# Near key tiles turned on VectorE instead of TensorE, with new orders in the first projections, the opening and the last pair

## What is computed

```python
x = x + xattn(layernorm(x), ctx, Wq, Wk, Wv, Wo)

def xattn(latents, context, Wq, Wk, Wv, Wo):            # 128 x 512, 2048 x 512
    hidden = concatenate([context, latents], axis=1)     # 2176 rows = 17 key tiles of 128
    q = (latents @ Wq).reshape(b, q_len, 4, 8, 128)      # 4 kv heads, 8 query heads each
    k = (hidden @ Wk).reshape(b, kv_len, 4, 128)
    v = (hidden @ Wv).reshape(b, kv_len, 4, 128)
    attn = softmax(einsum("bqhgd,bkhd->bhgqk", q, k) / sqrt(128))
    return einsum("bhgqk,bkhd->bqhgd", attn, v).reshape(b, q_len, 4096) @ Wo
```

## Time and profile before

| | |
|---|---|
| median of 3 runs | 638.62 us (638.28 to 638.98) |
| profiled execution, its time | 638.21 us |
| span, first to last instruction | 636.5 us |
| granted TensorE clock, mean | 0.999 of full |
| PE busy | 623.0 us (98%) |
| DVE busy | 434.4 us (68%) |
| ACT busy | 337.5 us (53%) |
| POOL busy | 212.9 us (33%) |

### The profile page before, as it was taken

How to read it: one execution, slowest core, us unless ns; L and a number is a source line. 1 busy time by engine, 2 the same in 40 slices (tenths; PEclk the granted TensorE clock), 3 DMA queues, 4 the chain that set the end, 5 groups by cost and what they waited for, 6 DMA issues and landing times.

```text
span 636.5 us, 11116 instructions
## 1 busy us (share of the span) xinstructions
PE 623.0 (98%) x3968; PEld 531.6 (84%) x3968; DVE 434.4 (68%) x885; ACT 337.5 (53%) x617; POOL 212.9 (33%) x161
## 2 busy tenths in 40 slices
PE   8999999999999999999999989999999999999998
PEld 6888887888999899889998879998879778797573
DVE  3533135686777777778876669789884775958873
ACT  3413114668776777777777636656454454447110
POOL 0000000349676867687765522225022020200000
PEclk9999999999999999999999999999999999999999
DMA  8501012467777767776756939475866757697500
GB/s 265 214 0 34 1 55 66 103 176 205 191 192 191 190 165 179 188 203 156 214 137 168 355 133 267 160 304 195 295 210 255 265 204 262 246 367 289 217 1 18
DMA packets 29534, 116.69 MB, mean 183 GB/s; under 512 B 7680, under 2 KB 8064, under 8 KB 21936
## 3 DMA queue, kind: packets, MB, share of 16 engines
q1 hardware_dynamic: 28912, 115.03, 57.7%
q10 hardware_dynamic: 576, 1.05, 0.6%
HBM read 86.30 MB, written 0.26 MB: 136 GB/s over the span
## 4 chain that ended last, share of the span: by engine, by line
PE 84%; DVE 6%; issue 2%; ACT 2%; DMA 2%; SPq 2%; POOL 1%; ACTq 0%; DVEq 0%
PE ps L1716 20%; PE ps L1434 13%; PE ps L1436 12%; PE ps L1435 12%; PE ps L1756 9%; PE ps L1508 4%; PE ps L1591 2%; PE ps L1745 2%; PE ps L1866 2%; DVE prob_far L1081 2%; DMA ring<-ctx_t_dram 2%; SPq L351 2%; PE ps L1829 2%; DVE prob_far L1109 2%; DVE res L1121 1%
## 5 line engine op out<-in xcount | busy, mean ns | idle before, releaser
L1716 PEld LDWEIGHTS ps<-norm_t,ring 128*128 128x128 f32 x1152 | 131.6, 192 | 4.9 <-issue 4.1
L1716 PE MATMUL ps<-norm_t,ring 128*128 128x128 f32 x1152 | 133.2, 276 | 0.0
L507 POOL TENSOR_TENSOR pt_lo<-far_t,pt_hi 128x512 fp32r<-128x512 f32 x86 | 102.2, 1203 | 61.6 <-ACT pt_hi L609 61.3
L1265 DVE SCALAR_TENSOR_TENSOR acc<-raw,cw,acc 128x127 f32<-128x127 f32 (+2 forms) x240 | 83.4, 424 | 18.8 <-ACT acc L879 18.2
L1081 DVE TENSOR_SCALAR_CACHE_REDUCE prob_far<-ps 128x1024 f32<-128x1024 f32 x64 | 73.8, 1155 | 31.9 <-PE ps L1436 31.6
L686 ACT ACTIVATE prob_far<-prob_far,neg_max 128x1024 f32<-128x1024 f32 x64 | 69.8, 1091 | 25.7 <-DVE neg_max L1085 25.6
L609 ACT ACTIVATE pt_hi<-far_t 128x512 fp32r<-128x512 f32 x90 | 51.3, 587 | 36.7 <-PE ps L1436 33.9
L1109 DVE STREAM_TRANSPOSE prob_far<-prob_far 128x1920 f32<-128x1920 f32 x30 | 65.0, 2171 | 0.1
L1434 PE MATMUL ps<-k_hi,q_hi 128*128 128x512 f32 (+2 forms) x160 | 62.4, 390 | 2.0 <-DVE prob_far L1081 1.6
L1434 PE MATMUL ps<-pt_hi,v_hi 128*128 128x256 f32 x208 | 61.1, 294 | 2.1 <-POOL pt_lo L507 1.2
L583 POOL TENSOR_SCALAR_AFFINE_SELECT at_hi<-a_hi 128x2048 fp32r<-128x2048 f32 x8 | 16.1, 2011 | 133.9 <-PE ps L1728 102.8
(11 more groups left out here) (213 smaller groups left out, 1213.8 us busy)
## 6 DMA issues: line engine op xcount, KB each, us to landing
ring<-w_in_dram SPq DMA_DIRECT2D x36, 1024.0 KB, 4.9
far_t<-prob_far SPq DMA_DIRECT2D x240, 120.0 KB, 2.3
ring<-w_out_dram SPq DMA_DIRECT2D x16, 1024.0 KB, 4.8
ring<-wq_dram SPq DMA_DIRECT2D x16, 512.0 KB, 4.2
ring<-wo_dram SPq DMA_DIRECT2D x16, 512.0 KB, 3.6
w_sb<-w_dram SPq DMA_DIRECT2D x4, 896.0 KB, 9.1
ring<-ctx_t_dram SPq DMA_DIRECT2D x3, 1024.0 KB, 6.9
ring<-w_dram SPq DMA_DIRECT2D x3, 1024.0 KB, 7.5
```

The source lines that it names most:

```text
L507: sub = lambda dst, a, hi: pool.tensor_tensor(dst, a, hi, ALU.subtract)
L1265: ins = nc.vector.scalar_tensor_tensor(a[:, i, back:], r[:, i, 0:T - back], cw[:, bass.ds(tile + i, 1), 3 - back:4 - back].rearrange("p a ...
L1716: ins = mm(ps[:, bank, t * T:t * T + T], w[:, t, c, :], norm_t[:, c, :], start=(c == 0), stop=(c == NC - 1))
```

## The change

All 17 key tiles, near ones too, are turned by VectorE and moved by DMA: `FAR_T` goes from 15 to 17, `turn_far` covers 2176 columns and waits for all three exponentials of its head, and `transposes`, both `near_split`s and the `near` tiles are gone. Units are renumbered: 0 and 1 are the plain tiles 13 to 16, which need only the move; 2 to 8 are split ones, on four slots in turn. GpSimd has seven remainders a pair, but VectorE takes unit 5 in the first step of a head (from n = 4 on) and unit 7 in the second. The orders on TensorE, ScalarE and VectorE change: the first exponential piece of the second head comes last on ScalarE, after the rounding of q; the first scores piece of pair n + 2 is evacuated in step n behind a block transpose; two chunks of scores lead in front of unit 0. `moves(m)` waits for TensorE's values of pair m - 2.

In the opening, the values of the last context block are made one tile at a time between the scores of pairs 0 and 1, and the latents' values come last. For the first context block VectorE rounds the context while ScalarE rounds Wk, TensorE does all high products first, and four more identity matmuls are made once the first quarter has landed. The first values are made in three passes over four banks. Cut to its core (removed helpers and buffers left out):

```diff
-FP32_TILES = {1: (13, 14), 2: (15, 16)}
+FP32_TILES = {0: (13, 14), 1: (15, 16)}
-FAR_T = (KV_LEN - NEAR) // P
+FAR_T = NKT
-SCORES_LEAD = {1: (2,)}
-SCORES_AT = {0: (1,), 2: (3, 4), 3: (5,), 4: (6, 7), 5: (8, 9)}
-LAST_SCORES_AT = {0: (1,), 2: (3, 4, 5), 3: (6, 7, 8, 9)}
+SCORES_LEAD = {0: (1, 2)}
+SCORES_AT = {1: (3, 4), 2: (5,), 3: (6, 7), 4: (8, 9)}
+LAST_SCORES_AT = {1: (3, 4, 5), 2: (6, 7, 8, 9)}
+LOW_U = {0: 5, 1: 7}
+SLOTS = 4
+WARM_SPLIT = 4
+def slot_of(p, u):
+    return (FAR_UNITS * p + u - FAR0) % SLOTS
+def by_dve(n, u):
+    return n > 0 and LOW_U.get(n % PAIRS) == u
 # SP, moves(m)
                 if m >= 2:
-                    sp.wait_ge(pfl_ok, FAR_UNITS * (m - 1))
+                    sp.wait_ge(pv_ps, UNITS * (m - 1))
+                elif m == 1:
+                    sp.wait_ge(kv_ps, 34)
 # GpSimd, a step
-                far_split(n, 3)
-                far_split(n, 4)
+                for u in (2, 3, 4):
+                    far_split(n, u)
+                if p == 0 and kv:
+                    v_split(kv, 2)
+                else:
+                    far_split(n, 5)
                 if n:
                     wo_split(n - 1, n - 1)
-                far_split(n, 5)
...
-                far_split(n, 7)
+                if p != 1:
+                    far_split(n, 7)
 # ScalarE, a step (the new order)
+                first_fars(n, kv, p)
                 if not begin:
                     output_split(n, b)
+                far(n, p, 4)
+                far(n, p, 5)
+                if not begin:
+                    wo_split(n - 1, 2 * kv + (p - 1) // 2, (p - 1) % 2)
...
                 soft_exp(n + 2, b, 0, 1)
+                if ask:
+                    far(n, p, 6)
...
+                soft_exp(n + 2, b, 0, 2)
+                soft_exp(n + 2, b, 0, 0)
+                far(n, p, 7 if ask else 6)
...
+                if ask:
+                    far(n, p, 8)
...
+                soft_exp(n + 2, b, 1, 1)
+                if not ask:
+                    far(n, p, 7)
...
                 soft_exp(n + 2, b, 1, 2)
+                if ask:
+                    q_split(n + 3, 1 - b, 6 + (1 - b))
+                soft_exp(n + 2, b, 1, 0)
...
+                if p == 3:
+                    act.wait_ge(pv_ps, 9 * n + 6)
+                    v_split(kv + 1, 1)
                 if not ask:
-                    soft_exp(n + 2, b, 1, 0)
+                    far(n, p, 8)
 # VectorE
-                dve.wait_ge(exp_ok, 2 * NPC * m + 3 * h + 2)
+                dve.wait_ge(exp_ok, 2 * NPC * m + 3 * h + 3)
...
                 turn_far(n + 1, 1 - b, 1)
+                scores_out(n + 2, b, 0, 0, sent)
...
                 scores_out(n + 2, b, 0, 2, sent)
-                scores_out(n + 2, b, 1, 0)
+                scores_out(n + 2, b, 1, 0, sent)
+                if p == 0 and not (isinstance(n, int) and n == 0):
+                    far_split(n, p, LOW_U[0])
                 scores_out(n + 2, b, 1, 1, sent)
                 scores_out(n + 2, b, 1, 2, sent)
-                if not ask:
-                    near_split(n + 1)
+                if p == 1:
+                    far_split(n, p, LOW_U[1])
                 if ask:
                     turn_far(n + 2, b, 0)
                     q_split(n + 3, 1 - b, 6 + (1 - b))
-                    near_split(n + 1)
-                    scores_out(n + 3, 1 - b, 0, 0)
 # TensorE, first block
+            pe.wait_ge(first_in[0], 32)
+            for _ in range(WARM_SPLIT):
+                mm(ps[:, 7, 0:P], ident[:], ident[:], start=True, stop=True)
             for c in range(NC):
+                pe.wait_ge(first_hi, c + 1)
+                pe.wait_ge(first_ctx, c + 1)
+                first_keys(c, wk_hi, ctx_hi[0], c == 0, False)
+                pe.wait_ge(first_lo, 2 * c + 1)
+                first_keys(c, wk_lo, ctx_hi[0], False, False)
                 pe.wait_ge(first_lo, 2 * c + 2)
-                for kv in range(KVH):
-                    ins = keys(0, kv, c)
+                first_keys(c, wk_hi, ctx_lo[0], False, c == NC - 1)
 # TensorE, opening
                 scores(0, 0, c)
-            project_values(3)
+                if c == 4:
+                    project_values(3, (0,))
+            project_values(3, (1,))
+            pe.wait_ge(ql_ok, 2)
+            for c in range(10):
+                scores(1, 1, c)
+                if c == 4:
+                    project_values(3, (2,))
+            project_values(3, (3,))
+            pe.wait_ge(v_ev, 14)
+            queries(2, 1, 0, 5)
...
             pe.wait_ge(v_ev, 17)
-            transposes(0, 0)
```

More of the change, by code:

```diff
@@ L315, in piece_banks, with plain @@
             return 2 * ((3 * h + i) % 2)
-        def plain(m, i):
-            return i == 0 or isinstance(m, int) and m == LAST_PAIR
+        def plain(m):
+            return isinstance(m, int) and m == LAST_PAIR
         def piece_ps(m, h, i):
@@ L559, in _ @@
                     v_split(kv + 1, 1)
-            for u in range(3, 5):
+            for u in range(2, 5):
                 far_split(LAST_PAIR - 1, u)
@@ L639, in split_ctx, with v_out @@
                 copy(ctx_hi[j % 2][:], ring[s][:].rearrange("p (c n) -> p c n", c=NC)).then_inc(c_hi, 1)
-            def v_out(j):
-                for t in range(4):
+            def v_out(j, tiles=range(4)):
+                for t in tiles:
                     act.wait_ge(kv_ps, 8 * j + 5 + t + (j == 3))
@@ L721, in output_split @@
                 o_split(1 - b)
-            def last_fars(n, b):
-                for u in range(6, 9):
-                    act.wait_ge(pv_ps, 9 * n + u - 2)
-                    far_split(b, u)
             def attn_step(n, kv, p):
@@ L828, in _ @@
             q_split(1, 1, 6)
+            act.wait_ge(v_ev, 8)
+            v_split(0, 0)
+            v_split(0, 1)
             for h in range(2):
@@ L831, in _ @@
                     soft_exp(0, 0, h, i)
[L832 removed]
+                v_out(3, (h,))
+                if h == 0:
+                    act.wait_ge(v_ev, 13)
+                    v_split(0, 2)
+            for h in range(2):
+                for i in (1, 2, 0):
+                    soft_exp(1, 1, h, i)
+                v_out(3, (2 + h,))
+            q_split(2, 0, 5)
             act.wait_ge(kv_ps, 34)
             copy(v_all[:, 16, :], ps[:, 4, :]).then_inc(v_ev, 1)
[L835 to L844 removed]
             attn_step(0, 0, 0)
@@ L1078, in scores_out @@
                 dve.wait_ge(s_ps, 6 * m + 3 * h + i + 1)
-                if i and not (isinstance(m, int) and m < 2):
+                if not (isinstance(m, int) and m < 2):
                     dve.wait_ge(moved[b], MOVED * before)
@@ L1453, in project_keys, with project_values @@
                     ins.then_inc(kv_ps, 1)
-            def project_values(j):
+            def project_values(j, tiles=range(4)):
                 ch, cl = ctx_hi[j % 2], ctx_lo[j % 2]
                 pe.wait_ge(w_lo, 1)
-                for t in range(4):
+                for t in tiles:
                     if j:
@@ L1554, in last_output @@
                 mm(ps[:, bank, :], o_l, last_wo_hi[:, h, :], start=False, stop=True).then_inc(wo_ps, 1)
-            def transposes(m, b):
-                pe.wait_ge(exp_ok, 2 * NPC * (m + 1))
-                if not (isinstance(m, int) and m == 0):
-                    pe.wait_ge(ptl_ok, m)
-                for w in range(2):
-                    for h in range(2):
-                        at = w * 256 + h * P
-                        ins = nc.tensor.transpose(ps[:, 4, at:at + P], near[b][:, h, w * P:w * P + P], ident[:])
-                ins.then_inc(t_ps, 1)
             def values(n, kv, b, u, fresh):
                 dst = ps[:, 6 + b, 0:2 * P]
-                slot = u % 3 if u else NEAR_SLOT
+                slot = slot_of(n, u)
                 if u == 0:
-                    pe.wait_ge(ptl_ok, n + 1) if n < LAST_PAIR else pe.wait_ge(last_lo, 1)
                     if n:
@@ L1681, in _ @@
             ins.then_inc(kv_ps, 1)
-            pe.wait_ge(ql_ok, 2)
-            for c in range(6):
-                scores(1, 1, c)
             pe.wait_ge(v_ev, 17)
-            transposes(0, 0)
-            queries(2, 1, 0, 7)
-            for c in range(6, 10):
-                scores(1, 1, c)
             for n in range(LAST_PAIR - 1):
```

269 lines of the change are left out of this document (120 added, 149 removed).

## The result

The median of 3 runs is 628.63 us (627.82 to 628.82), against 638.62 before: 10.0 us less, a ratio of 0.984 with a 95% interval of 0.9822 to 0.9857. The profiled execution took 628.63 us (span 626.9) against 638.21 (636.5). The forecast was 629.9 and faster; its range holds the result. Five later runs of the same kernel gave 628.79. The clock may have a small share in the difference of the medians: of 39 other executions of the kernel before, 20 had a mean granted clock of 0.994 to 0.997 (all 39 have a median of 638.8, the 19 without it 638.4), and none of the eight of the kernel after had. The two profiled executions, at 0.999 and 1.000, differ by 9.6 us.

The account below looks back on a forecast made before the run. TensorE was taken as the bound (84% of the chain that ended last). Gains of 1.1 + 2.4 + 4.1 + 0.1 + 1.0 = 8.7 us gave 629.5 us for the profiled execution, 629.9 at the median; range 626.3 to 634.7.

Parts of the forecast that it names:

- The first 20 us: Start, first context block: parallel roundings, high products first; first product at 8.0, values at 19.0; gain 1.1 us (0.5 to 1.6).
- The opening: 92.8 to 134.7 us: value products spread between scores cover VectorE's evacuations and transposes; gain 2.4 us, between 1.0 and 2.7.
- The 0.7 us wait for the latent's values: Opening, before step 0: TensorE waits for the copy of the latent's values, now uncovered; an added cost of 0.7 us.
- A group of transposes: Near transposes leaving TensorE: 0.36 us for each of 15 groups, 5.4 us; a step goes from 16.09 to 15.73.
- Waits in the steady part: Twelve steady steps: TensorE waits of 1.5 + 1.2 + 0.9 = 3.6 us, from unit 6, third scores pieces and other steps.
- transposes alone are 4.3: Steady part, 195.8 to 191.7 us: gain 4.1, of which transposes alone are 4.3, so the waits roughly stay.
- The end: After the steady part: net 0.1 us from steps 12 and 13, 1.0 from the last step, where plain tiles come first.
- VectorE's block transposes: Near tiles turned on VectorE: 2176 columns take 2.38 us, 0.28 more, twice a pair, hidden with 0.3 us to spare.
- The lock: VectorE instructions with two SBUF inputs and GpSimd ones reading SBUF exclude each other; a VectorE remainder costs 0.69 to 1.9 us.
- rival A: Steady part: lock and GpSimd's queue cost double, waits of 7 us instead of 3.6; 633.3 to 634.7 us; chance 0.25.
- Rival B: Steps: DMA moves become the bound, TensorE waiting at unit 0; slower, 642.7 us at L = 17; chance 0.08.
- Rival C: Steps: no gain, VectorE's loop takes 0.9 us longer, each of 14 steps losing 0.6; 638.3 us; chance 0.05.

Follow-up runs that it names:

- experiment 5: Kernel after with the opening's order on TensorE, ScalarE and VectorE as before, still without the near transposes: 633.76 us.
- experiment 1: Kernel after with a group of four unused 128x128 identity transposes put back on TensorE at each of 15 places: 630.97 us, ratio to before 0.9886.
- experiment 6: Kernel after with unit 6's remainder earlier on GpSimd and, in a head's first step, unit 6 rounded before the exponentials on ScalarE: 626.13 us.
- experiment 3: Kernel after with the first context block's roundings, warm-up and TensorE order of products as before: 630.28 us.

## Why the prediction was right

The direction, the size, the range and the forecast's own bounds (626 to 632.5) hold. The sum is closer than its terms: the first 20 us and the opening came 0.8 us under the forecast, the steady part and the end 1.7 over, and that these errors partly cancel is luck. Its steps:

- **The first 20 us: 1.1.** In the profiles 0.7; by the runs that undo it 1.5. Right within what can be told, but not by the working's path. The first product came at 7.45 instead of 8.0, and the values at 19.59 instead of 19.0: 12.1 us for the 48 products and not 11.0, since TensorE waited 0.84 us for the second slice's rounding, whose load had landed late. The unchanged kernel run again waited 0.45 at the fourth slice instead. The working has the loads in time everywhere.
- **The opening: 2.4.** Measured 2.0 against the kernel before. The working prices the order alone; by experiment 5 the order has a second worth that it doesn't name, as the old one would now cost 5.0 us. The 0.7 us wait for the latent's values is where it was put:

```profile
120.61 0.39 PE L1444 MATMUL ps<-k_hi,q_hi 128*128 128x256 f32 x1 [0.69 <-ACT v_all L638]
```

- **A group of transposes: 0.36.** It is 0.46 of a clean step; the term left out the slower first matmul behind the group. The period without waits is 15.48, not 15.73: my 16.09 for the step before held 0.15 of late starts that I took for the step itself (16.09 less 0.46 is 15.63).
- **Waits in the steady part: 3.6.** 5.3 (190.35 less 185.05, which is twelve times 15.48 less the 0.7 of the first). The places are those of the text, the sizes are not: unit 6 in a head's first step 0.95 instead of 0.5, the 0.46 by which GpSimd's wo remainder is longer beside VectorE's (2.86 for 2.40), the third piece after a head's second step 0.4 to 0.5 as written, 0.3 in the second steps that I had at 0.15. Gain 5.5 against 4.1: the shorter period gives 3.0 more (12 x 0.25), the waits take 1.7 back. That is 0.44 us of waits a step, under the 0.6 that was to refute the forecast.
- **What I had wrong without harm** is where the steady gain comes from. The text says that transposes alone are 4.3 and the waits roughly stay. As a balance that is so: with 15.94 for a clean step that has a group, the kernel before has 5.2 us of waits (195.8 less 190.6), the kernel after 5.3, and the gain is the twelve groups, 5.5. As a cause it is not: experiment 1 says that the rest of the change took 3.7 us of waits away, and that the transposes, 5.5 us of TensorE's time, give 1.8, as waits grow into the room. That what was taken away and what grew back are equal is luck; the working has neither.
- **The end: 1.1** (0.1 and 1.0). Measured 1.4. The wait at 366.52 is gone; units 7 and 8 of step 13 are late by 0.2 each (forecast 0.3). No run undoes this part alone:

```profile
338.89 0.39 PE L1444 MATMUL ps<-pt_hi,v_hi 128*128 128x256 f32 x1 [0.22 <-DVE pt_lo L996]
340.80 0.38 PE L1444 MATMUL ps<-pt_hi,v_hi 128*128 128x256 f32 x1 [0.23 <-POOL pt_lo L534]
```

- **VectorE's block transposes.** 2437 ns against the estimate of 2.38 us, hidden in the clean steps as said. The rule of the Trainium skill (VectorE: DVE Perf Modes, Rules for kernel authors), which gives 128x128 transposes to TensorE, would have kept them there; put back on TensorE as transposes of the identity, they cost 2.2 us net (experiment 1). Here the engine that the rule wants to load is the full one.
- **The lock.** A VectorE remainder cost 0.93 in a head's first step and 1.82 in the second, and GpSimd's went from 1.3 to 1.74 (experiment 6) beside it. It is the cost of rival A in a single instruction; in the sum, 5.3 us of waits lie between the forecast's 3.6 and the rival's 7.
- **Rival B** did not come, and its chance of 0.08 was fair for the wrong reason. 17/15 of the bytes left the issue at 0.59 us and the landing at 2.6 for 2.3; the number of DMAs is what counts, and the margin is about 1 us, against ScalarE's use, rather than the 0.2 to 4 that I had from TensorE's.
- **Rival C** did not come: VectorE takes the 256-column piece out in 0.42 us in both kernels (at 114.06 before, at 109.82 after), runs of 32 or not.

## What to carry to other kernels

Where several engines run a few tenths of a microsecond behind the full one, work taken off the full engine can be worth less than its time (1.8 of 5.5 us here) until the queues behind it are shortened too; count the waits from starts, not from the idle column. The deadline of a transfer is that of its first reader on any engine, not that of the engine which bounds the kernel. Undo an order on all engines together: one engine's half of it measured 9 us where the whole measured 5.

## What the runs showed of the hardware

- After 5.4 us without work TensorE's granted clock was 0.50 for some 5.5 us, and after 1.8 us idle at the start it was 0.50 for about 3 us; a wait of 1.44 at the same place in the profiled execution of the kernel before left it at 1.00. The same kernel does not always do the same: the mean clock was 0.997 in three executions of experiment 3's kernel and 0.999 and 1.000 in two, and below 0.999 in 20 of 39 of the kernel before. After the 5.4 us wait that cost an estimated 2.8 us more, about half as much again.
- An SBUF-to-SBUF DMA of 136 KB takes 0.59 us to issue (median), one of 120 KB the same, and with halves among them the median is still 0.59. From the start of a group to its end it is 0.65 us each for 16, and 0.67 and 0.68 for 20 and 24, no less for being smaller.
- A VectorE subtraction with two SBUF inputs and a GpSimd one stretch each other: 1.82 for 0.69 on VectorE, 1.74 for 1.3 and 2.86 for 2.4 on GpSimd.
